# First fill issued by two engines, row maxima taken in pairs over four banks in the two lone batches, and chunks that start two places later

## The reference

```
Q, K, V = (einsum('oc,bct->bto', W, x).split_heads(16) for W in (Wq, Wk, Wv))   # x: 8 x 256 x 512
att = (Q @ K^T) / 4 + b;  att = att * m + (1 - m) * -1e30;  att = softmax(att)
y   = (att @ V) -> 8 x 256 x 512                                                # rows t of 512 features
Wg, Wu (4096 x 512), Wd (512 x 4096) = 4-bit codes looked up, times a scale per block of 32
out = x + (gelu(y @ Wg^T) * (y @ Wu^T)) @ Wd^T
```

## Time and profile before

| | |
|---|---|
| median of 3 runs | 1525.85 us (1523.91 to 1530.12) |
| the profiled execution | 1526.61 us, its span 1524.8 us |
| PE busy | 1421.5 us, 93% of the span |
| DVE, ACT, POOL busy | 698.3 us, 752.1 us, 309.6 us |
| mean granted TensorE clock | 0.966 of full |
| up to the first maximum tile | 40.3 us |
| batches 0 and 1 | from about 62 us to about 206 us |
| first matmul of chunks 0, 1, 2, 3 | 221.8, 576.9, 924.7 and 1257.9 us |

### The profile page before, as it was taken

One profiled execution on the slowest core, in us unless ns is written; L12 is line 12 of the kernel. 1 busy time (PEld: TensorE's weight loads), 2 busy tenths in 40 slices (PEclk: granted clock), 3 DMA queues, 4 the chain that ended last, 5 costly groups with the idle time before them and its releaser, 6 DMA issues.

```text
span 1524.8 us, 18901 instructions
## 1 busy us (share of the span) xinstructions
PE 1421.5 (93%) x7376; PEld 555.1 (36%) x7376; DVE 698.3 (46%) x934; ACT 752.1 (49%) x855; POOL 309.6 (20%) x242
## 2 busy tenths in 40 slices
PE   3688779999999998999999998999999999999998
PEld 1122223333333333333433333333333334444443
DVE  5667668777778753433344333433343111111111
ACT  2255558666667663555665554556655631111110
POOL 3002024433444421111211111111111111111110
PEclk7589989999999999999999999999999999999999
DMA  5130324443354332432243320432222223233220
GB/s 182 51 87 15 101 78 163 154 131 122 108 183 157 133 125 65 143 99 84 84 128 106 101 84 20 155 119 83 84 84 83 84 83 138 83 126 123 83 84 28
DMA packets 51129, 157.91 MB, mean 104 GB/s; under 512 B 7632, under 2 KB 21072, under 8 KB 50912
## 3 DMA queue, kind: packets, MB, share of 16 engines
q1 hardware_dynamic: 48192, 153.80, 29.5%
q10 hardware_dynamic: 2848, 2.90, 0.6%
HBM read 118.64 MB, written 37.77 MB: 103 GB/s over the span
## 4 chain that ended last, share of the span: by engine, by line
PE 81%; DMA 4%; DVE 3%; ACT 3%; issue 3%; POOL 2%; SPq 2%; ACTq 1%; POOLq 0%; DVEq 0%
PE psum L896 14%; PE psum L897 13%; PE psum L898 13%; PE psum L944 8%; PE psum L945 7%; PE psum L946 7%; PE psum L866 7%; PE psum L852 4%; PE psum L836 4%; PE psum L812 2%; DMA wide<-seed_rows 2%; POOL dq_w L400 1%; DVE w_ring L414 1%; PE psum L822 1%; ACTq L393 1%
## 5 line engine op out<-in xcount | busy, mean ns | idle before, releaser
L633 ACT ACTIVATE big<-psum 128x1024 f32<-128x1024 f32 x256 | 260.1, 1024 | 328.4 <-PE psum L852 321.4
L896 PE MATMUL psum<-y_hi,w_ring 128*128 128x512 f16 x1024 | 390.5, 381 | 16.5 <-POOL y_lo L515 15.8
L898 PE MATMUL psum<-y_hi,w_ring 128*128 128x512 f16 x1024 | 389.6, 380 | 0.0
L897 PE MATMUL psum<-y_lo,w_ring 128*128 128x512 f16 x1024 | 389.4, 380 | 0.0
L700 DVE TENSOR_REDUCE maxima<-psum 128x2 f32<-128x1024 f32 x179 | 219.2, 1225 | 253.6 <-PE psum L836 253.3
L527 POOL TENSOR_TENSOR in_lo<-inter,in_hi 128x512 f16<-128x512 f32 x128 | 150.4, 1175 | 811.1 <-ACT in_hi L615 810.5
L748 DVE SCALAR_TENSOR_TENSOR inter<-psum,gelu 128x512 f32<-128x512 f32 x128 | 88.2, 689 | 315.4 <-PE psum L898 301.4
L944 PE MATMUL psum<-w_ring,in_hi 128*128 128x512 f16 x512 | 195.5, 382 | 7.7 <-ACT gelu L608 4.3
L945 PE MATMUL psum<-w_ring,in_hi 128*128 128x512 f16 x512 | 194.8, 380 | 0.0
L946 PE MATMUL psum<-w_ring,in_lo 128*128 128x512 f16 x512 | 194.6, 380 | 0.0
L896 PEld LDWEIGHTS psum<-y_hi,w_ring 128*128 128x128 f16 x1024 | 100.1, 98 | 202.6 <-issue 82.7
(11 more groups left out here) (69 smaller groups left out, 987.3 us busy)
## 6 DMA issues: line engine op xcount, KB each, us to landing
w_ring<-w_parts SPq DMA_DIRECT2D x96, 768.0 KB, 7.2
w_parts<-w_ring SPq DMA_DIRECT2D x32, 768.0 KB, 3.3
dq_scales<-scales SPq DMA_DIRECT2D x32, 384.0 KB
wide<-qk_parts SPq DMA_DIRECT2D x64, 128.0 KB
qk_parts<-wide SPq DMA_DIRECT2D x60, 128.0 KB
dq_packed<-packed SPq DMA_DIRECT2D x32, 192.0 KB
small<-x SPq DMA_DIRECT2D x8, 512.0 KB, 6.6
wide<-qk_parts SPq DMA_DIRECT2D x64, 64.0 KB
```

The source lines that it names most:

```text
L633: nc.scalar.activation(p_exp[:, k, :, i], p_score[:, bank:bank + 2, :], ACT.Exp, scale=SCORE_SCALE).then_inc(exp_done, 1)
L896: nc.tensor.matmul(dst, w[:, 0, k % 2, cols], hi, start=(k == 0), stop=False)
L897: nc.tensor.matmul(dst, w[:, 0, k % 2, cols], lo, start=False, stop=False)
L898: return nc.tensor.matmul(dst, w[:, 1, k % 2, cols], hi, start=False, stop=(k == TT - 1))
```

## The change

1. **Start.** The rest of the mask is no longer loaded: eight per-batch flags (`any_b`) go to DRAM and come back broadcast. The loads of packed weights move behind the first quad's `move_max`. ACT runs a dummy copy first, which takes its table load early. The first fill is split: SP issues the half e = 0, ACT the half e = 1, both ahead of the load of the second `x`. The fill of unit 1 follows as soon as the first has landed (step F1 is gone). The casts of V and `x` move behind ACT's half.
2. **Lone batches.** PLAN gets the order of SHARED_PLAN without its places. Maxima are taken in pairs, in banks 2, 3 and 4, 5 by turns; scores have banks 0 and 1 only, so each pair of score matmuls waits for the exponential before it. F0 moves from quad 2 to the start of quad 1, G1 from the end of quad 3 to the start of quad 2. Unit 0 is decoded in batch 0, units 1 and 2 in batch 1.
3. **Chunks** start behind the second `|` after that YN; two empty places are added at the end of attention.
4. **Down product.** It waits for each unit's `in_lo` instead of all four, and the last one of all runs unit by unit over the four output banks instead of bank by bank.

```diff
-        p_score, p_max, p_av, p_misc = psum[:, 0:4, :], psum[:, 4:6, :], psum[:, 6, :], psum[:, 7, :]
+        p_score, p_av, p_misc = psum[:, 0:2, :], psum[:, 6, :], psum[:, 7, :]
+        def max_bank(n, b_now):
+            return 2 if b_now < SOLO and n // 2 % 2 else 4
...
         PLAN = (
-            "F1 A2 m A3 m AO m S00 S01 V1a m m S10 V1b V1h m S11 m Y S20 MT MH XH YN m m ML S21 MV A0 m m A1 m "
-            "S30 m S31 m Q0a m Q0b m Q0h Q0l",
-            "X A2 m S00 m d0 K0a K0b m K0h S01 m S10 m A3 K0l AO m m S11 Y m MT MH ML S20 MV m S21 m Q1a YN m Q1b "
-            "Q1h m S30 Q1l A0 m m A1 m S31 m",
-            "S00 K1a m S01 m K1b K1h m S10 m F0 K1l S11 m A2 m d1 A3 MT AO m MH m S20 ML Y m S21 MV m V0a YN m "
-            "S30 m S31 A0 m m A1 m m",
-            "S00 m S01 d2 m A2 m m V0b S10 V0h m m A3 m AO S11 m MT m S20 m Y YN MH m ML U G1 S21 MV m S30 A0 m S31 m "
-            "A1 m wh m wl",
+            "S00 m m A2 V1a S01 m m A3 V1b V1h AO S10 m m XH S11 m m d10 MT Y MH ML YN d11 S20 m m A0 Q0a MV d12 S21 m m "
+            "Q0b Q0h h1 S30 m m A1 Q0l K0a S31 m m K0b K0h K0l l1",
+            "X F0 S00 m m A2 Q1a S01 m m A3 Q1b Q1h AO S10 m m Q1l S11 m m MT Y MH ML YN S20 m m A0 MV K1a S21 m m "
+            "K1b K1h S30 m m A1 K1l S31 m m",
+            "G1 S00 m m A2 d00 d20 S01 m m A3 AO S10 m m d01 d21 S11 m m MT Y MH ML YN d02 d22 S20 m m A0 MV L2 S21 m m V0a "
+            "S30 m m h0 h2 A1 V0b V0h S31 m m l0 l2",
+            "S00 m m A2 S01 m m A3 AO S10 m m S11 m m MT Y MH ML YN S20 m m A0 MV L3 S21 m m S30 m m A1 S31 m m",
         )
...
-            for step in "| A2 | A3 | AO | | Y | YN".split():
+            for step in "| A2 | A3 | AO | | Y | YN | |".split():
...
-                for r in range(4):
-                    for i in range(GROUP):
+                for i in range(GROUP):
+                    for r in range(4):
                         yield STEPS, "D", (STEPS // GROUP - 1, r, i)
...
-            ready = [n + 1 for n, (b, g, step, _) in enumerate(steps) if step == "YN" and g == 0 and b >= 2 and b % 2 == 0]
+            ready = []
+            for n, (b, g, step, _) in enumerate(steps):
+                if step == "YN" and g == 0 and b >= SOLO and b % 2 == 0:
+                    places = [m for m in range(n, len(steps)) if steps[m][2] == "|"]
+                    ready.append(places[1] + 1)
...
+            sp.wait_ge(dve_own, 2)
+            sp.dma_start(any_dram, any_b).then_inc(any_out, 16)
...
             store_qk(sp, 0, 0, 0)
-            store_qk(sp, 0, 0, 1)
+            sp.wait_ge(seed_out, 16)
+            sp.wait_ge(qk_out[0], 64)
+            fill_half(sp, 0, 0, 0, 0)
+            store_qk(sp, 0, 1, 0)
+            store_qk(sp, 0, 1, 1)
+            sp.wait_ge(stack_in[0], 16 * STACK_DMAS)
+            fill_stack(sp, 0, 0, 1, False)
...
             move_max(sp, 0, 0, 0)
+            load_unit(sp, 0)
+            load_unit(sp, 1)
...
+            for side in range(2):
+                qk_part(0, side, 0, True, psum[:, side, :])
+            store_qk(act, 0, 0, 1)
+            for side in range(2):
+                qk_part(0, side, 1, True, psum[:, 2 + side, :])
+            for i in range(3):
+                act.wait_ge(proj_in[i], 16)
+                nc.scalar.activation(w_parts[i][0], w_proj[i], ACT.Copy, scale=W_SCALE).then_inc(wp_hi_s, 1)
+            act.wait_ge(seed_out, 16)
+            act.wait_ge(qk_out[0], 64)
+            fill_half(act, 0, 0, 0, 1)
...
-                if b_now < SOLO or n % 2 == 0:
-                    wait_from(pe, max_red, 16 * (4 * b + g) + n - (1 if b_now < SOLO else 0))
+                if n % 2 == 0:
+                    wait_from(pe, max_red, 16 * (4 * b + g) + n - (2 if b_now < SOLO else 0))
...
-                wait_from(pe, exp_done, n - 1 if b < SOLO else n)
-                bank = 2 * i if b < SOLO else 0
+                wait_from(pe, exp_done, n)
...
+                if r == 0:
+                    pe.wait_ge(in_lo_s, u + 1)
                 if i == 0:
-                    if r == 0:
-                        pe.wait_ge(in_lo_s, GROUP * j + GROUP)
```

More of the change, by code:

```diff
@@ L240, in plan @@
                     continue
-                if step == "F1" and not first:
+                if step[0] in "dhl" and (step[1] == "0") != first:
+                    continue
+                if step == "L2" and not first or step == "L3" and first:
                     continue
@@ L522, in _ @@
             x_low(0)
-            weight_f(pool, 0)
             def inter_low(u):
@@ L540, in _ @@
                     x_low(b + 1)
-                elif step == "d2" and b < SOLO:
-                    weight_f(pool, b + 1)
+                elif step in ("d02", "d12", "d22") and b < SOLO:
+                    weight_f(pool, int(step[1]))
         @block.scalar
@@ L591, in _ @@
             x_high(0)
[L592 to L597, removed]
             max_part(0, 0, True)
@@ L621, in _ @@
                         inter_high(u - 1)
-                    elif step == "G1" and SOLO < u + AHEAD_UNITS - 1 < UNITS:
+                    elif step == "G1" and AHEAD_UNITS <= u + AHEAD_UNITS - 1 < UNITS:
                         weight_hi(act, u + AHEAD_UNITS - 1)
@@ L649, in _ @@
                     x_high(b + 1)
-                elif step == "wh" and b < SOLO:
-                    weight_hi(act, b + 1)
+                elif step in ("h0", "h1", "h2") and b < SOLO:
+                    weight_hi(act, int(step[1]))
         @block.vector
         def _(dve):
+            nc.vector.memset(act_warm[:, :], 0.0).then_inc(warm_in, 1)
             for e in range(2):
@@ L699, in reduce_pair @@
                 dve.wait_ge(max_mm, 16 * q + n + 2)
-                nc.vector.reduce_max(maxima[:, g % 2, n // 2:n // 2 + 9:8], p_max, AX.X).then_inc(max_red, 2)
+                nc.vector.reduce_max(maxima[:, g % 2, n // 2:n // 2 + 9:8], psum[:, bank:bank + 2, :],
+                                     AX.X).then_inc(max_red, 2)
             def max_part(b, g):
@@ L765, in _ @@
                         decode(dve, n, int(step[1]))
-                    elif step == "G3" and SOLO < n - 1 < UNITS:
+                    elif step == "G3" and AHEAD_UNITS <= n - 1 < UNITS:
                         weight_lo(dve, n - 1)
@@ L786, in _ @@
                 elif step[0] == "d" and b < SOLO:
-                    decode(dve, b + 1, int(step[1]))
-                elif step == "wl" and b < SOLO:
-                    weight_lo(dve, b + 1)
+                    decode(dve, int(step[1]), int(step[2]))
+                elif step in ("l0", "l1", "l2") and b < SOLO:
+                    weight_lo(dve, int(step[1]))
         @block.tensor
@@ L847, in scores @@
                     pe.wait_ge(max_in, 16 * MAX_DMAS * (4 * b + g) + 16 * MAX_DMAS)
-                wait_from(pe, exp_done, n - 1 if b < SOLO else n)
-                bank = 2 * i if b < SOLO else 0
+                wait_from(pe, exp_done, n)
                 for e in range(2):
                     rows, s = slice(HALF * e, HALF * e + STACK_ROWS), 2 * g + i
-                    last = nc.tensor.matmul(p_score[:, bank + e, :], k_stack[rows, side, s, k * P:(k + 1) * P],
+                    last = nc.tensor.matmul(p_score[:, e, :], k_stack[rows, side, s, k * P:(k + 1) * P],
                                             q_stack[rows, side, s, :], start=True, stop=True)
```

101 lines of the change are left out of this document (42 added, 59 removed).

## The result

The changed kernel takes 1517.71 us (median of 8 runs, 1509.06 to 1521.37), the kernel before 1524.88 us in the same comparison (8 runs, 1521.34 to 1530.12): ratio 0.9936, 95% interval 0.9918 to 0.9954. It is faster by 0.64%, not by the 1.7% forecast, and the time lies 2.7 us outside the range. The profiled execution took 1521.37 us, its span 1519.5, its mean TensorE clock 0.967. In three of the kernels further down, four executions (1537, 1842, 2396 and 3616 us) ran at another level than the rest of their kernel; the medians and ratios leave them out.

The account below looks back on a forecast made before the run. Behind 222 us only PE's waits and slow-clock stretches can be won, before that a chain bounds it. Terms -7.3 - 4.5 + 10 - 5 - 14.4 - 4.4 = -25.6 from 1526.6 give 1501.0, forecast 1500, range 1484 to 1515.

Parts of the forecast that it names:

- Phase: Two places' shift changes which step meets which; chunk 0's 14.3 us of small waits may halve or grow by half: 0 +- 5.
- Chunks 1, 2 and 3: Chunk starts: all three y_lo waits go, and the slow stretch in chunks 1 and 2: -14.4 us (-9 to -15).
- Start: Up to the first maximum tile: earlier first fill, tile at 33.0 instead of 40.34 us: -7.3 (-4 to -10).
- first scores: From first maximum tile to first scores: paired maxima and the move take 17.5 us, not 21.95: -4.5 (-2.5 to -5.5).
- Lone batches: Batches 0 and 1: fill waits go, single score banks and clock cost more, 154 us against 143.8: +10 (+3 to +22).
- batch 2's quad 0: Up to chunk 0's first product: -5 us (-1 to -6), of which -2.2 for full instead of half clock.
- rival 1: Scores' single banks cost less than summed; lone batches take 130 to 135 us, giving -10, time 1480; chance 0.14.
- Rival 2: Idling PE keeps lone batches at half clock: 1559 us if throughout; chance 0.04 slower than before, 0.12 half of it.
- The end: Last down product: its 2.72 us in_lo wait is covered and the slow stretch goes: -4.4 us (bound -3).
- rival 3: Waits at chunk starts only move, or new ones open in chunks 1 and 2; 14 us not gained, 1514; chance 0.08.

Follow-up runs that it names:

- the lag alone: Changed kernel with all chunks back at their old start, but chunk 0 handing out two steps at 22 places instead of 16: 1520.96 us, ratio 0.9963.
- first_chunk_four_places: Changed kernel with chunk 0 starting four places behind YN instead of two, chunks 1 to 3 as changed: 1513.08 us, ratio 0.9913.
- late_start_old_phase: Changed kernel with late chunk starts kept, but chunk 0 handing out two steps at its first 10 places, then three: 1490.83 us, ratio 0.9782.
- chunks_old_place: Changed kernel with all chunks starting directly behind YN again, all else as changed: 1499.86 us, ratio 0.9837.
- first_fill_one_issuer: Changed kernel with chunks at their old places and SP issuing both halves of the first fill, ACT none: 1509.41 us, ratio 0.9868.
- first_chunk_old_place: Changed kernel with only chunk 0 starting directly behind YN, chunks 1 to 3 still two places later: 1509.75 us, ratio 0.9888.
- the last two kernels: Changed kernel, late starts kept, chunk 0 with ten places of two steps, then three: 1490.83 us; the same with the cast of x behind YN: 1488.23 us.

## Why the prediction was wrong

**Phase, the step that failed.** It saw that the shift changes which step meets which, and priced that at 0 ± 5 us from the 14.3 us of idle time that chunk 0 had, "may halve or grow by half". It more than doubled (14.3 to 32.0 us), and the clock went with it: like for like the row lost 24.6 us, and that is net of what the chunk's start gave (its wait for `y_lo` fell from 4.75 to 1.13). That the phase is the cause is shown: the lag alone gives +16.9 us (357.7 to 374.5), and taking only the lag out gives -21.5 in the stage, though the six steps stand in it again, and, by the two ratios, 0.0154 of 1525, or 23.5 us, in the whole. Between the stretches 205.97 to 583 and 208 to 565 shown above lie 20.0 us, of which 13.6 are idle time of PE (32.0 to 18.4) and 6.4 busy time, at clocks of 0.97 and 0.99. The lower clock is a cost of its own and not the same each time: `first_chunk_four_places` has the changed kernel's waits (34.3 us in the stage, 33.7 there), a clock of 0.982 instead of 0.964, and 4.7 us less.

The reading went wrong in taking the present idle time as the scale. It says how well the old order happened to fit, not what a worse one costs. My reading is that this hangs on the slack of the queues behind it. In chunk 0 DVE is busy 256 and ACT 234 of 348 us, and each waits for POOL's 3.12 us conversions ahead of steps that PE needs at once; in chunk 1, with 38% and 57% and no conversions, the same shift by six steps cost 2.5 us. No run varies the slack alone. Which meeting costs how much stays open too: moving the weight chain moved the wait.

**Chunks 1, 2 and 3** (-14.4). The waits all went: behind 584 us PE has only this one.

```profile
PE psum L904 <- ACT gelu L633: 3.2, 10, 0.3
```

The quads with the chunk starts fell from 49.3 to 43.9, -5.4 each for the -5.85 forecast. But 2.5 us were lost over chunk 1's other seven quads, and here the kernel before had no wait for gelu; that is the new phase, by all likelihood. Chunk 3's start gave 1.6 of 2.7. In all about -9.7 (-3.0, -5.1 and -1.6): the term was mis-sized, just inside its bound of -9. That late places cost nothing by themselves is shown by `late_start_old_phase`: its median of 1490.8 is 9 us below that of `chunks_old_place`.

**Start** (-7.3, measured -9.5) and **first scores** (-4.5, measured -5.9). SP's first issue came at 19.55, not 18.5, and ACT's at 19.57, as forecast. From there to the tile 11.3 us passed, not 14; the 2 us for SP's stores behind its half look like too much. The -9.5 is close to the -9.8 that the prediction named for a fill bound by issue, so the number alone would point at the wrong mechanism. `first_fill_one_issuer` tells the two apart: the fill is bound by what the transfers take. The Trainium skill (DMA: Bandwidth & Descriptors, Issuing engines are not separate DMA queues) says the same; the run agrees, 30.58 us with one issuer and 30.87 with two, though the last issue came at 24.10 instead of 22.00. The move of the maxima took 4.9 us (41.93 to 46.8) instead of 6.0.

**Lone batches** (+10, measured -0.4 with batch 2's quad 0, for which the forecast sum was +7.8). The pitch of scores was what it was taken for, and PE does stand for ACT there, as these groups of 46.87 to 192 us show (busy, mean ns, idle before and releasers):

```profile
L717 DVE TENSOR_REDUCE maxima<-psum 128x2 f32<-128x1024 f32 x64 | 78.0, 1224 | 44.9 <-PE psum L845 44.9
L657 ACT ACTIVATE big<-psum 128x1024 f32<-128x1024 f32 x64 | 65.6, 1025 | 59.6 <-PE psum L860 59.6
L860 PE MATMUL psum<-wide 53*128 53x512 f16 x128 | 28.6, 442 | 27.2 <-ACT big L657 22.7 <-DMA wide<-max_lo 4.2
```

The fills are gone from the list, where one of batch 1 stood 6.0 us. What I oversized is the projections' share: I added them to a base quad of 16.0 one after another, but they fit into gaps. In the trace where these batches had the best clock (0.91, `first_chunk_old_place`) the seven quads from Y to Y took 14.4, 15.9, 15.9, 21.4, 14.7, 15.6 and 16.1 us, and the stretch 140.6: there rival 1 came true, with 13.5 us less than before. **Rival 2**, the clock, came true in part: it was 0.80 and 0.87 in the changed kernel's profiled execution, and the stretch took 13 us longer. That the row came out near zero is a meeting of these two errors.

**The end** (-4.4) was right to the tenth, and **rival 3** came nearest to what happened. But it looked for the new waits in chunks 1 and 2, and put the loss at 14 us; they came in chunk 0.

The errors partly cancelled. With the phase's loss taken out, the changed kernel gains 33 us (2.2%) where the sum said 25.6: the other terms together were too cautious by 8 us, and the phase alone put the time outside the range.

## What to carry to other kernels

Where several in-order queues are interleaved by hand, a shift of one list against another is an edit in itself. Don't price it by the idle time that the tuned order has left; look at how much slack the queues have at the densest stage, and leave room for a loss larger than all of that idle time (here offsets of three and six steps cost 7 to 30 us of 355, where 14 were idle). A share handed out as "what is left over the places left" moves its phase whenever an end moves; keep the phase by writing the counts out, as ten twos and then threes do here. Last, take such a pair apart by a run: up to the last two kernels every late start here brought the lag with it, and parting them turned 0.6% into 2.2%.

## What the runs showed of the hardware

The lone batches drew different clocks from run to run with the same instructions in them. These are the windows 46.87 to 80, to 120, to 160 and to 187 us, first of the changed kernel, then of `first_chunk_old_place`, which differs only from batch 2 on (the clock is the third number from the right):

```profile
46.87:80.00 33.13, 27.28 (x147) 7.32 (x147) 19.84 (x23) 17.12 (x21) 3.19 (x3) 0.76 0.46 123
80.00:120.00 40.00, 29.98 (x197) 6.86 (x193) 29.75 (x34) 24.13 (x27) 5.87 (x5) 0.84 0.17 46
120.00:160.00 40.00, 31.37 (x178) 8.03 (x174) 26.15 (x31) 21.25 (x26) 7.42 (x6) 0.79 0.20 54
160.00:187.00 27.00, 18.04 (x138) 5.22 (x142) 20.53 (x26) 16.71 (x20) 5.10 (x4) 0.94 0.55 171
```

```profile
46.87:80.00 33.13, 27.85 (x159) 8.00 (x158) 20.93 (x25) 19.25 (x24) 3.19 (x3) 0.82 0.43 123
80.00:120.00 40.00, 29.19 (x235) 8.76 (x227) 31.16 (x36) 26.22 (x31) 6.16 (x6) 0.96 0.18 45
120.00:160.00 40.00, 30.97 (x190) 7.39 (x190) 32.71 (x43) 23.12 (x29) 9.24 (x9) 0.87 0.28 78
160.00:187.00 27.00, 18.23 (x158) 5.62 (x155) 19.08 (x19) 17.71 (x20) 3.76 (x3) 1.00 0.39 138
```

The one reached Y of batch 2 quad 0 at 200.6 us, the other at 187.3. PE is busy some three quarters of such a stretch and idle mostly for under 2 us at a time (once 3.5, for moved maxima), and the clock falls and rises between its two levels. In the traces of the thirteen kernels that run these two batches as the changed kernel does (it among them), the stretch from the first scores to Y of batch 2 quad 0 took 140.6 to 155.7 us. That is as wide as the spread of one kernel's runs (1487.9 to 1501.1), and may well be its source; it isn't shown, with one trace for each kernel. It is why a difference below some 5 us was read from the stages rather than from the medians. The Trainium skill (TensorE: Matmul & The Clock Gate, A second HAM failure mode: psum-queue depth-cycling) describes short idles between groups of matmuls as enough for the clock to swing; these windows agree, with 0.76 to 1.00 for like work.
